# A gated attention layer and a mixture of eight experts in one program: three reorderings and an early ScalarE table load

## The reference

```python
mod = (silu(c) @ wmod).reshape(32, 6, 1, 128)           # sa, ca, ga, sb, cb, gb
h = layernorm(x) * (1 + ca) + sa                        # x: 32 x 256 x 128
K = exp(h @ Wk1.T + bk1); S = cumsum(K * h) / (cumsum(K) + 1e-6)
O_ar = S * sigmoid(h @ Wq1.T + bq1)
E = h[t] - O_ar[t-1]                                    # zero at t = 0
K2 = sigmoid(0.02 / sqrt(128) * (h[t-1] @ Wk2.T + bk2))
O_ma = cumsum(K2 * E) * Q2[t-1]
x = x + ga * ((O_ar + O_ma) @ Wproj.T + bproj)
h = layernorm(x) * (1 + cb) + sb
e = argmax(h @ centroids.T)                             # one of 8 experts a row
y = h + relu(ln_e(h) @ W1[e] + b1[e]) @ W2[e] + b2[e]   # hidden width 512
x = x + gb * y
```

## Time and profile before

| | us |
|---|---|
| median of three executions | 351.2 (351.09 to 355.27) |
| the profiled execution | 351.7 |
| its span on the core | 350.0 |

### The profile page before, as it was taken

How to read it: one execution, slowest core, us unless ns; L and a number is a source line. 1 busy time by engine, 2 the same in 40 slices (tenths; PEclk the granted TensorE clock), 3 DMA queues, 4 the chain that set the end, 5 groups by cost and what they waited for, 6 DMA issues and landing times.

```text
span 350.0 us, 8167 instructions
## 1 busy us (share of the span) xinstructions
PE 299.8 (86%) x1824; PEld 229.7 (66%) x1824; DVE 272.0 (78%) x939; ACT 246.3 (70%) x537; POOL 235.4 (67%) x370
## 2 busy tenths in 40 slices
PE   4866979898989989889788999999999998999930
PEld 4333546465546646555466999899999988888820
DVE  5598899999999999799775377998666656666650
ACT  2678699988888998889756667666766766666400
POOL 7982236669878787888478867878877554454470
PEclk9989699999999999999898999999999999999975
DMA  7232386425449984464485879877777788785000
GB/s 203 90 113 75 105 251 159 120 92 173 132 142 206 263 215 166 80 130 150 135 272 176 251 252 297 268 223 224 228 222 217 206 225 232 217 226 172 31 16 0
DMA packets 49429, 60.86 MB, mean 174 GB/s; under 512 B 5557, under 2 KB 38095, under 8 KB 49379
## 3 DMA queue, kind: packets, MB, share of 16 engines
q1 hardware_dynamic: 42806, 43.11, 47.0%
q0 software_dynamic: 6368, 16.82, 13.4%
q10 hardware_dynamic: 208, 0.41, 0.3%
HBM read 39.90 MB, written 20.87 MB: 174 GB/s over the span
## 4 chain that ended last, share of the span: by engine, by line
PE 55%; DVE 16%; issue 13%; ACT 7%; SPq 2%; DMA 2%; DVEq 1%; ACTq 1%; POOL 1%; POOLq 0%
PE bank L806 15%; PE bank L779 11%; PE bank L783 5%; DVE shared L1165 3%; PE bank L732 3%; PE bank L711 3%; PE bank L723 3%; PE bank L708 2%; PE bank L684 2%; PE bank L661 2%; PE bank L749 2%; PE bank L703 2%; ACT shared L897 2%; PE bank L792 2%; DVE xbn L1062 1%
## 5 line engine op out<-in xcount | busy, mean ns | idle before, releaser
L591 POOL DMA_INDIRECT out_dram<-shared,ids x71 | 71.8, 1012 | 45.9 <-DVE shared L1627 28.9
L516 POOL DMA_INDIRECT expert_rows<-rows,slots x64 | 64.8, 1013 | 18.9 <-issue 14.4
L806 PE MATMUL bank<-w_all,shared 128*128 x568 | 72.5, 279 | 2.6 <-issue 1.0
L806 PEld LDWEIGHTS bank<-w_all,shared 128*128 128x128 f32 x568 | 66.9, 192 | 6.3 <-issue 6.2
L974 ACT ACTIVATE shared<-bank,par 128x256 f32<-128x256 f32 x100 | 40.9, 470 | 22.3 <-PE bank L779 22.2
L779 PE MATMUL bank<-shared,early 128*128 128x256 f32 x200 | 49.3, 391 | 2.3 <-ACT shared L1006 2.3
L479 POOL TENSOR_SCALAR zz<-rows,negm,rstd 128x128 f32<-128x128 f32 x64 | 30.9, 491 | 25.1 <-ACT rstd L956 19.8
L779 PEld LDWEIGHTS bank<-shared,early 128*128 128x128 f32 x200 | 36.9, 195 | 7.1 <-ACT shared L1006 2.9
L1439 DVE TENSOR_TENSOR shared<-bank,b_bc 128x256 f32<-128x256 f32 (+1 forms) x46 | 15.8, 362 | 29.1 <-PE bank L806 18.4
L471 POOL TENSOR_SCALAR xh<-x_in,negm,rstd 128x128 f32<-128x128 f32 x64 | 30.6, 488 | 11.2 <-DVE shared L1138 10.8
L1006 ACT ACTIVATE shared<-bank,par 128x256 f32<-128x256 f32 (+1 forms) x46 | 22.6, 514 | 8.2 <-issue 5.1
(11 more groups left out here) (209 smaller groups left out, 673.3 us busy)
## 6 DMA issues: line engine op xcount, KB each, us to landing
early<-in_L_ffn_W_dram SPq DMA_DIRECT2D x25, 256.0 KB, 3.7
x_in<-expert_rows SPq DMA_DIRECT2D x15, 385.0 KB, 4.1
rows<-in_L_ffn_W_dram SPq DMA_DIRECT2D x21, 256.0 KB, 3.2
x_in<-in_L_attn_x_dram SPq DMA_DIRECT2D x16, 256.0 KB, 3.5
rows<-gates_rows SPq DMA_DIRECT2D x32, 128.0 KB, 4.9
full<-expert_rows SPq DMA_DIRECT2D x10, 385.0 KB, 4.7
expert_rows<-pad_rows SPq DMA_DIRECT2D x9, 385.0 KB, 9.1
full<-expert_rows SPq DMA_DIRECT2D x11, 192.5 KB, 3.1
```

The lines of the kernel that those rows point to most:

```text
L516: pool.indirect_dma_start(rows_dram, bass.IndirectOffsetOnAxis(ap=slots[:, c * CN + t:c * CN + t + 1], axis=0), rows[:, c % RR, t, :], Non ...
L591: pool.indirect_dma_start(out_rows, bass.IndirectOffsetOnAxis(ap=ids[:, u % IR, t:t + 1], axis=0), u_sb[:, k, t, :], None, bounds_check=T - 1,
L806: mm = pe.matmul((ps_q, ps_k)[k][:, t * D:(t + 1) * D], hid[:, k, f, t * P:(t + 1) * P], of_expert(w2_all, e, f * D, (f + 1) * D), start=( ...
```

## The change

- ACT: behind the second tanh of each chunk but the last, the logarithm's table is loaded at once (`preload_act_table_set`), so that none is loaded ahead of L904.
- ACT takes over the negated means (`minus_means`, behind L947 and in `rstd_of`); DVE keeps only those of the first four chunks.
- Beginning: ACT scales the first hT before it copies the biases, and no longer waits for `bproj`; DVE takes the statistics of chunks 3 and 4 one place earlier.
- Step 15: DVE takes the statistics of expert tiles 0 and 1 and normalises both within the step; ACT makes their reciprocal deviations and their L1006, and PE transposes both, before the hidden layer of tile 0.
- Blocks: PE reads the experts of two blocks a tile from j = 14 on (`of_blocks`), instead of one before each block's output.
- DVE: the loop over `plan_blocks` runs over nothing for j below 7. In the kernel before, its range starts at 5*(j-7) and ends at 0 there, so that it calls `plan_blocks` with 40 negative numbers at j = -1, 35 at j = 0 and so on to 5 at j = 6; each call makes no instruction but the wait of `ready()`.

```diff
+                if q < NC - 1:
+                    act.preload_act_table_set("natural_log")
...
-            act.wait_ge(s_small, 16 * 4)
...
+            def minus_means(i, kinds):
+                if i == 4:
+                    act.wait_ge(s_negm, 4)
+                act.activation(negm[:, i, kinds, :], mv[:, i, kinds, :, 0], ACT.Copy, scale=-1.0).then_inc(s_negm, 1)
...
+                if c == NC - 1:
+                    tile_stats(0)
+                    tile_means(0)
...
-                for part in range(5 * (j - 7), min(5 * (j - 6), 28) if j >= 7 else 0):
+                for part in range(5 * (j - 7), min(5 * (j - 6), 28)) if j >= 7 else ():
                     plan_blocks(part)
...
-            turn_tile(0)
+            turn_tile(1)
             for j in range(0, NJ + 1):
                 if in_b(j):
                     hidden(j)
-                if in_b(j + 1):
+                if in_b(j + 1) and j > 0:
                     turn_tile(j + 1)
...
                     expert_out(j - 1)
+                if j == NF - NB // FS - 1:
+                    pe.wait_ge(s_planned, 4)
+                if NF - NB // FS - 1 <= j:
+                    for b in range(len(of_blocks), min(len(of_blocks) + 2, NB)):
+                        of_blocks.append(expert_of(pe, NF + b // FS, b % FS))
```

More of the change, by code:

```diff
@@ L342, in _ @@
                 sp.dma_start(bias_raw[:, n:n + 1], v.rearrange("(p o) -> p o", o=1)).then_inc(s_small, 16)
-            sp.dma_start(bproj_bc[:, :], bproj.partition_broadcast(B)).then_inc(s_small, 16)
+            sp.dma_start(bproj_bc[:, :], bproj.partition_broadcast(B)).then_inc(s_params, 16)
             for c in range(4, 6):
@@ L687, in logits @@
                 if z == 6:
-                    pe.wait_ge(s_params, 48)
+                    pe.wait_ge(s_params, 64)
                     for n in range(NV):
@@ L921, in tanhs, with rstd_of_tile @@
                 act.activation(ps_q[:, :], ps_q[:, :], ACT.Tanh, bias=bias[:, 1:2], scale=0.5).then_inc(s_tq, 1)
+                if q < NC - 1:
+                    act.preload_act_table_set("natural_log")
+            def rstd_of_tile(v):
+                n = len(parts(v))
+                act.wait_ge(b_aggr, rows_so_far(v))
+                wait(act, b_rstd, v - 3)
+                act.activation(blnv[:, v % 4, 0:n], bmv[:, v % 4, 0:n, 1], ACT.Ln, bias=epsv[:, :]).then_inc(b_lnv, 1)
+                act.wait_ge(b_lnv, v + 1)
+                wait(act, b_z, FS * (v - 3))
+                act.activation(brstd[:, v % 4, 0:n], blnv[:, v % 4, 0:n], ACT.Exp, scale=-0.5).then_inc(b_rstd, 1)
             for c in range(-2, NC):
@@ L931, in _ @@
                 if c == -2:
+                    act.wait_ge(s_small, 16 * 3)
+                    act.copy(bias[:, 0:1], bias_raw[:, 0:1]).then_inc(s_bias, 1)
+                    act.mul(bias[:, 1:2], bias_raw[:, 1:2], 0.5).then_inc(s_bias, 1)
+                    act.mul(bias[:, 2:3], bias_raw[:, 2:3], 0.5 * MA_K * ISQ).then_inc(s_bias, 1)
+                    act.wait_ge(s_bias, 3)
                     act.wait_ge(s_gate, 1)
@@ L938, in _ @@
                     turned_z(z)
+                if c == NC - 1:
+                    rstd_of_tile(0)
+                    rstd_of_tile(1)
                 if in_a(q):
@@ L948, in _ @@
                                    ).then_inc(s_lnv, 1)
+                    minus_means(i, kinds)
                 if in_a(q):
@@ L985, in relu_of_blocks @@
                     r.then_inc(b_hidA, 1)
-            def rstd_of_tile(v):
-                n = len(parts(v))
-                act.wait_ge(b_aggr, rows_so_far(v))
-                wait(act, b_rstd, v - 3)
-                act.activation(blnv[:, v % 4, 0:n], bmv[:, v % 4, 0:n, 1], ACT.Ln, bias=epsv[:, :]).then_inc(b_lnv, 1)
-                act.wait_ge(b_lnv, v + 1)
-                wait(act, b_z, FS * (v - 3))
-                act.activation(brstd[:, v % 4, 0:n], blnv[:, v % 4, 0:n], ACT.Exp, scale=-0.5).then_inc(b_rstd, 1)
             def norm_of_expert(n):
@@ L1013, in _ @@
             turned_z(NC - 3)
-            rstd_of_tile(0)
             rstd_of(NC - 2)
+            experts = [norm_of_expert(0)]
             sum_of(NC - 1)
-            experts = norm_of_expert(0)
-            rstd_of_tile(1)
+            experts.append(norm_of_expert(1))
             rows_of(NC - 3)
@@ L1023, in _ @@
                     rstd_of_tile(j + 2)
-                now = experts
+                now = experts[j]
                 wait(act, b_y, j - 1)
@@ L1031, in _ @@
                     relu_of_blocks(j, now, 1)
-                if in_b(j + 1):
-                    experts = norm_of_expert(j + 1)
+                if in_b(j + 1) and j > 0:
+                    experts.append(norm_of_expert(j + 1))
                 if j >= NF:
@@ L1442, in _ @@
             ahead = 5
+            x_all(3)
             k_sum(0)
@@ L1446, in _ @@
             kv_sum(0)
-            x_all(3)
+            x_all(4)
             ratio(0)
@@ L1456, in _ @@
             kv_sum(1)
-            x_all(4)
             x_all(5)
@@ L1492, in _ @@
                     gated_error(c)
+                if c == NC - 1:
+                    tile_stats(1)
+                    tile_means(1)
                 if first:
@@ L1521, in _ @@
                 if c == NC - 1:
-                    dve.wait_ge(s_planned, 1)
-                    tile_stats(0)
-                    tile_means(0)
+                    dve.wait_ge(s_b2, 16)
+                    normalise_tile(0)
                 if turn:
@@ L1545, in _ @@
                         x_means(a, t)
-                if c >= 0 and (in_a(a) or in_a(o)):
-                    minus_means(c + 5, in_a(a), in_a(o))
-            dve.wait_ge(s_b2, 16)
-            normalise_tile(0)
-            tile_stats(1)
-            tile_means(1)
+            normalise_tile(1)
             for t in range(CN):
                 z_stats(NC - 1, t)
-            normalise_tile(1)
             for t in range(CN):
                 z_means(NC - 1, t)
-            minus_means(NC + 5, False, True)
             for j in range(-1, NJ + 2):
```

25 lines of the change are left out of this document (9 added, 16 removed).

## The result

| | before | changed |
|---|---|---|
| median, us (20 executions each) | 351.2 | 355.1 (353.25 to 357.64) |
| ratio to before | | 1.011, 95% interval 1.0086 to 1.0135 |
| span of the profiled execution | 350.0 | 353.4 |

The change makes the kernel 1.1% slower: clearly more than nothing, and within 2%. 355.3 had been predicted.

The account below looks back on a forecast made before the run. Half of the loop's chunks were taken to hang on ACT and PE, half on DVE and PE. 351.7 + 5.0 + 0.1 + 1.8 - 1.9 - 0.9 = 355.8, less 0.5 for the median: 355.3 us; ranges 350 to 358 and 346.0 to 360.0.

Parts of the forecast that it names:

- beginning: Start of the kernel: two ACT waits end (-0.97, -1.54), two more table loads (+2.60), +0.1 us; bounds -1.2 to +2.1.
- step 15: Loop's end: waits ahead of tile 1 go, earlier preparation, less added statistics, -1.9 us; bounds -3.0 to -0.5.
- blocks: Blocks: PE's expert reads, moved into the full tiles, no longer slow the last blocks, -0.9 us; bounds 0 and -1.5.
- Table load: Loop: load delays L897 by 0.63 us; six routed chunks pay 0.63, six others 0.2, +5.0; bounds +1.9 to +7.6.
- one fall of the clock: Routed chunks: PE drops once to its lower clock level behind L661's longer idle, +1.8 us; bounds 0 to 11.
- Negated means: Loop: moving 0.20 us a chunk from DVE to ACT gives 0; up to -2.4 if DVE sets the cycle.
- The first side: Beginning: ACT's 0.97 us wait for bproj goes, and the 1.54 ahead of L947 may go too.
- The second: Beginning: two more table loads, since the exponentials undo the first chunks' preloads, 2 x 1.30 us.
- rival C: Full tiles: PE's added expert reads are exposed, up to 0.9 us a tile, so 365 us; chance 0.05.
- B: Loop: PE's clock falls in most chunks; three more falls than the sum has give 360.7 us; chance 0.13.
- D: Loop: load stays hidden, DVE sets the cycle with 0.20 us less a chunk, so 345.5 us; chance 0.20.
- E: Loop: the load drains as the skill page says, adding 16 us, so 371 us; chance 0.01.

Follow-up runs that it names:

- e3: The kernel before with only the range of plan_blocks mended, so no empty waits for j below 7: 350.1 us, 0.9964 of before.
- e8: The kernel before with only the new beginning (biases copied later, no bproj wait, earlier statistics of chunks 3 and 4): 350.77 us, 0.9938.
- e10: The changed kernel without the preload and with the negated means back on DVE: 347.46 us, 0.9902 of before.
- e1: The changed kernel without the table load behind the second tanh: 346.45 us, 0.9825 of before.
- e11: The changed kernel without the preload, run again as a comparison: 346.86 us, 0.9882 of before.
- e2: The kernel before with the table load behind the second tanh as its only edit: 358.61 us, 1.0181 of before.
- e4: The changed kernel with PE's reads of the blocks' experts put back before each block's output: 355.64 us, 1.0101 of before.
- e7: The changed kernel without the preload, both expert tiles' statistics in step 15 behind the product L1189: 344.74 us, 0.9837 of before.
- e9: The changed kernel with the load moved behind the copy of the sum L870, ahead of turned_z: 347.99 us, 0.9878 of before.
- e5: The changed kernel with three table loads behind the second tanh in place of one: 424.24 us (two executions).
- e6: The changed kernel with the load one place later, between L905 and the copy of the sum L870: 375.7 us, 1.0653 of before.

## Why the prediction was right, point by point

The direction and the main mechanism, the load on the chain, were right. That the time came out as near as 355.1 for 355.3 is luck: the terms have errors of both signs that cancel. By the landmarks of the two profiled executions:

| term | predicted | measured |
|---|---|---|
| beginning | +0.1 | -0.08 (scan 2) |
| loop: load, clock, means | +5.0, +1.8, 0 | +6.41 (scan 2 to 14) |
| step 15 | -1.9 | -2.65 (scan 14 to tile 1) |
| full tiles | 0 | -0.27 (tile 1 to 24) |
| blocks | -0.9 | +0.04 (tile 24 to the last store) |
| sum | +4.1 | +3.45 |

**Table load.** The mechanism was right: load on the chain, L905 0.64 us later behind the tanh (0.63 predicted), L661's idle at 1.85 (1.83), scans 10.96 apart in a routed chunk (10.8), a granted clock of 0.99 in the loop (0.95 or more). The term was +5.0 beside +1.8 for one fall of the clock, together 6.8. By the version without the preload it is 7.60 in the loop: 1.65 of it is the lower level behind the idle of 2.25 in step 2, and 5.95 the delay, 0.50 a chunk for the 0.42 taken on the mean. The 0.42 came from 0.63 in routed chunks and 0.2 in the others; by the scans it was 0.72 to 1.47 and nothing. The fall was predicted in one of the routed chunks, behind L661; it came at L723, in step 2, which has no L661 yet. The step "such an idle of 1.84 is followed by the lower level" was wrong for this place: six idles of 1.85 to 1.88 were not. At its own place, ahead of L708 in step 14, it held in each trace with 1.83 or 1.84 there (the kernel before, e3, e8, e10). The changed kernel has 1.34 there (175.29) and no fall: L711 takes 1.12 for 2.03 and L749 1.05 for 1.86. This fall that went away, 1.7 us on PE, is in no term; whether any of it reached the chain isn't shown.

**Negated means.** Put at 0, because DVE was not alone on the chain. With the preload in place this can't be read by itself, but the loop of the changed kernel grew by 6.41 only, 127.39 against 120.98, and without the preload it was 1.19 shorter than before. That is the first error: -1.2, or -2.5 by the version with the means back on DVE (of which 1.0 hangs on the new beginning), the size that was kept for the rival in which DVE sets the pace. DVE's work still counted in the chunks without idle on DVE, 0.14 to 0.21 each from step 7 to 12.

**Beginning.** +0.1 predicted, -0.08 measured. The first side held: the waits' end gives 2.75 to 3.25 at scan 2 (e1, e8, e11; 2.51 predicted). The second, 2.60 for two additional loads, measures 2.67 only by luck: in the kernel before the same loads cost 0.36 (e2), and in the changed one some 0.6 of the 2.67 is the next load, ahead of L905.

**Step 15.** -1.9 predicted. From scan 14 to tile 1's hidden layer the changed kernel takes 19.59 us, before 22.24: -2.65. The cost of the statistics ahead of the scan was seen, but as work (1.44), and the sum took 0.4 for it; the scan of step 15 comes 9.90 behind that of step 14, before 8.84, so it was 1.06. What DVE also does there is wait for the tiles' rows:

```profile
180.40 0.49 DVE L1411 BATCH_NORM_STATS2 bbn<-x_in 128x6 f32<-128x128 f32 x2 [0.69 <-DMA x_in<-expert_rows]
...
182.87 0.49 DVE L1411 BATCH_NORM_STATS2 bbn<-x_in 128x6 f32<-128x128 f32 x2 [0.26 <-DMA x_in<-expert_rows]
...
183.93 1.20 DVE L1183 TENSOR_TENSOR_SCAN shared<-seq_mask,bank 128x512 f32<-128x512 f32 x1
...
186.16 1.16 PE L749 MATMUL bank<-wg,Mp 128*128 128x128 f32 x8 [0.99 <-DVE Mp L1189]
...
189.19 1.89 PE L779 MATMUL bank<-shared,early 128*128 128x256 f32 x8
...
193.62 1.97 PE L779 MATMUL bank<-shared,early 128*128 128x256 f32 x8 [1.17 <-ACT shared L1002]
```

0.69 and 0.26 for the DMA, and PE's last projection waits 0.99 for the product. On the other side tile 0's hidden layer runs in 1.89 us, all at the upper level, where it had 3.47; that is 1.58 that no term had. It isn't this change's own. e4 has the same instructions in this stretch and its last scan at 183.91, yet PE ran at the lower level from L749 on, and tile 1's hidden layer came 1.54 later:

```profile
186.13 1.92 PE L749 MATMUL bank<-wg,Mp 128*128 128x128 f32 x8 [1.17 <-DVE Mp L1186]
...
191.16 2.88 PE L779 MATMUL bank<-shared,early 128*128 128x256 f32 x8
...
195.16 1.97 PE L779 MATMUL bank<-shared,early 128*128 128x256 f32 x8 [0.33 <-ACT shared L999]
```

From scan 14 to tile 1 that is 21.33 us, -0.91 against the kernel before. So one and the same code gives -2.65 or -0.91 by the level of the clock, and that -1.9 lies between them is luck. Without the preload the same layer takes

```profile
181.06 3.44 PE L779 MATMUL bank<-shared,early 128*128 128x256 f32 x8
```

and with the preload in the kernel before it takes 1.99 and the one of tile 1 3.49. The traces fit an order by the idle ahead of that L749: none, 0.99 and 1.06 (e7, the changed kernel, e10) had the upper level behind them, 1.17, 1.29, 1.83 and 2.00 (e4, e9, e1, e11) the lower. No run was made to isolate it.

**Blocks.** -0.9 predicted; nothing measured (60.29 us against 60.25, and the same from the blocks on with the reads put back). The step that failed is "if PE's reads made the 0.19 of difference": they didn't. PE's periods went from 4.57 to 4.48 on the mean, but stay at 4.50 with the reads put back (e4) and go to 4.52 with the range alone (e3). Nor is the time there set by PE: at the end it waits for ACT and DVE. This error of 0.9 and those of the means and of step 15 go opposite ways.

**Full tiles.** 0 predicted, -0.27 measured; the reads ahead are hidden, and the rival C fell: tiles from 14 on still follow each other every 3.7 to 3.8 us.

**The rivals.** B (the clock falls in most chunks) needed idles longer than the change makes: at 4.43 it did come true (e5), at 1.85 not. D (DVE's relief shows and the load is hidden) was half there: the relief showed, the load wasn't hidden. E, a drain behind the load, fell: in this trace, too, L905 starts 1.29 us behind the load's start. The Trainium skill ("ScalarE: Activation LUTs", section What ACT_TABLE_LOAD costs) gives 2.66 us with a drain; of that, the runs here show the 1283 ns of the load and no drain.

**The numbers of the rivals.** D's 345.5 takes the 0.5 off twice: its sum, 346.0, has it already. And the forecast has two ranges, 350 to 358 and, further on, 346.0 to 360.0; the measured time lies in both.

## What to carry to other kernels

A table load, or any fixed cost, is not cheaper for being issued early: ask what stands behind it on its engine, and who waits for that. Here the load had a free place (behind the last instruction that anyone waited for), and moving it to an apparent gap of 0.67 us ahead of a critical instruction cost about 0.5 us a round and 8 to 10 us in all, with the beginning and the lower clock, more than the other parts of the change had gained together (4 to 6). A change with several parts is worth taking apart: without the one that lost, and with one step moved, the kernel is 1.6% faster than before rather than 1.1% slower. A sum that comes out right can hold wrong terms: here the means were put at 0 and measured -1.2 or more, and the blocks at -0.9 and measured 0. And work moved into a busy stage should stand behind the instruction that others wait for, above all if it waits for a DMA itself.

## What the runs showed of the hardware

- PE's clock and idles, at 30 to 200 us: single idles of 1.20 (all kernels), 1.85 (the changed one, e2, e4), 2.79, 3.00 and 3.22 us (e5) ahead of L661 were followed by no slower matmul; 2.25 ahead of L723, and 3.43 and 4.43 ahead of L661 (e5), were followed by 1.5 to 2.1 us where the upper level takes 1.02 to 1.16. An idle of 1.60 ahead of L723 went either way, in two executions of one kernel too (e1 and e11). Of six pairs of 1.20 and 1.19 with 0.63 us of work between, five were followed by the lower level (e6). The length of one idle doesn't decide it.
- With the same code and DVE's scan at the same time, the level of PE's clock alone moved the hidden layer of tile 1 by 1.5 us (the changed kernel and e4).
- A table load takes 1.28 us, and the next instruction starts 1.29 to 1.30 behind its start, here too with the load ahead of an instruction that waits for another engine.
- Waits that are met long before aren't free: DVE's "issue" of 1.49 us, the place of 35 or 40 of them, went with the empty waits (e3), and 1.3 us of the time with it (interval 0.1 to 2.5).
